# First block of an embedding tower: eight table look-ups by one-hot matmul, half of them in float32 the first time, all tables loaded at once

## What is computed

```
e = stack([tbl_f[ids[:, f]] for f in range(26)], axis=1)
c = concatenate((dense[:, None, :], e), axis=1)          # 2048 x 27 x 128
pairs = einsum('bfd,bgd->bfg', c, c)[:, iu, ju]           # 351 per sample
h = concatenate([dense, pairs, dense], axis=1)
h = maximum(h @ W_top1 + b_top1, 0); h = maximum(h @ W_top2 + b_top2, 0); y = h @ W_top3
```

## Time and profile before

| | us |
|---|---|
| median of 3 runs | 412.22 |
| profiled execution | 411.75 |
| its span | 409.9 |
| PE busy | 380.7 |
| DVE busy | 244.0 |
| POOL busy | 275.5 |
| ACT busy | 221.1 |

### The profile page before, as it was taken

The page is one execution under the profiler, slowest core; times in us unless marked ns, Lnnn a source line. Parts: engine busy times, 40 slices in busy tenths (PEclk is TensorE's granted clock), DMA queues, the critical chain, the costliest instruction groups (busy, mean ns, idle before and its releaser), DMA issues.

```text
span 409.9 us, 8420 instructions
## 1 busy us (share of the span) xinstructions
PE 380.7 (93%) x3248; PEld 371.3 (91%) x3248; DVE 244.0 (60%) x684; ACT 221.1 (54%) x461; POOL 275.5 (67%) x296
## 2 busy tenths in 40 slices
PE   0396699999999999999999999999999999999996
PEld 0395699999999999999999999999999999999885
DVE  4599868375593847467484737657395747621422
ACT  2256276557375546647365546647464555637531
POOL 4777777777777777777777777777777777760000
PEclk9979999999999999999999999999999999999999
DMA  7986833323322333333332333333333332220000
GB/s 164 274 223 136 215 86 87 80 74 91 72 77 69 88 79 80 83 73 83 85 77 69 83 82 74 91 73 80 72 79 81 85 77 62 57 53 1 2 0 2
DMA packets 25732, 35.02 MB, mean 85 GB/s; under 512 B 8710, under 2 KB 19478, under 8 KB 25693
## 3 DMA queue, kind: packets, MB, share of 16 engines
q0 software_dynamic: 9216, 18.89, 19.3%
q1 hardware_dynamic: 14396, 15.45, 15.7%
q10 hardware_dynamic: 2080, 0.15, 0.4%
HBM read 34.45 MB, written 0.01 MB: 84 GB/s over the span
## 4 chain that ended last, share of the span: by engine, by line
PE 86%; DVE 5%; ACT 3%; DMA 2%; issue 1%; SPq 1%
PE look L442 28%; PE prod L469 27%; PE mlp L487 10%; PE turn L453 7%; PE mlp L498 6%; PE mlp L489 3%; DMA dense<-in_dense_rows 2%; DVE onehot L356 2%; PE mlp L506 2%; DVE table_lo L404 1%; ACT feats L280 1%; PE mlp L479 1%; ACT diag L295 1%; PE prod L548 1%; ACT table_hi L268 1%
## 5 line engine op out<-in xcount | busy, mean ns | idle before, releaser
L260 POOL DMA_INDIRECT rows<-in_tbl,ids x288 | 274.7, 954 | 91.3 <-issue 84.8
L356 DVE TENSOR_SCALAR onehot<-wanted,row_no 125x256 fp32r<-125x256 int32 x528 | 164.0, 381 | 18.8 <-PE look L442 18.3
L295 ACT ACTIVATE diag<-prod 32x216 f32<-32x216 f32 x256 | 87.6, 342 | 144.4 <-PE prod L469 142.2
L442 PE MATMUL look<-onehot,table_hi 125*128 125x256 f32 x528 | 137.4, 297 | 23.0 <-DVE table_lo L404 18.3
L442 PE MATMUL look<-onehot,table_lo 125*128 125x256 f32 x528 | 131.9, 287 | 0.0
L469 PE MATMUL prod<-feats 128*128 128x108 f32 x1024 | 124.1, 274 | 1.8 <-ACT feats L280 1.1
L442 PEld LDWEIGHTS look<-onehot,table_hi 125*128 125x128 f32 x528 | 103.1, 195 | 24.6 <-issue 24.6
L469 PEld LDWEIGHTS prod<-feats 128*128 128x128 f32 x1024 | 119.5, 192 | 2.6 <-ACT feats L280 1.4
L442 PEld LDWEIGHTS look<-onehot,table_lo 125*128 125x128 f32 x528 | 103.4, 196 | 0.0
L379 DVE TENSOR_SCALAR h<-mlp,b_sb 128x128 f32<-128x128 f32 x90 | 26.0, 344 | 128.2 <-PE mlp L489 83.4
L280 ACT ACTIVATE feats<-turn 128x512 f32<-128x512 f32 (+1 forms) x80 | 78.4, 1021 | 1.4 <-PE turn L453 0.2
(11 more groups left out here) (39 smaller groups left out, 89.6 us busy)
## 6 DMA issues: line engine op xcount, KB each, us to landing
wanted<-in_small_ids SPq DMA_DIRECT2D x64, 128.0 KB, 3.4
rows<-in_tbl,ids POOLq DMA_INDIRECT x288
feats<-in_tbl SPq DMA_DIRECT2D x7, 448.0 KB
dense<-in_dense_rows SPq DMA_DIRECT2D x16, 64.0 KB, 3.3
w_sb<-in_w_pairs SPq DMA_DIRECT2D x1, 702.0 KB
feats<-in_tbl SPq DMA_DIRECT2D x1, 560.0 KB
w_sb<-in_w SPq DMA_DIRECT2D x1, 512.0 KB
feats<-in_tbl SPq DMA_DIRECT2D x7, 52.0 KB
```

Of the source, the lines that this page charges most:

```text
L260: gp.indirect_dma_start(rows[:, q % SLOTS_OF_ROWS, f * D:(f + 1) * D], None, large_tables[g + f], bass.IndirectOffsetOnAxis(ap=ids[:, t, g ...
L295: last = nc.scalar.activation(diag[t % 2][W * i:W * (i + 1), s * SEG_GROUPS * SLOTS:(s + 1) * SEG_GROUPS * SLOTS], prod_part(prod[s % 2], ...
L356: made = nc.vector.tensor_scalar(onehot[v % 2][:, c - row_nos_at(h), :], wanted[v % WANTED][0:CP, :], row_no[:, c:c + 1], None, ALU.is_equal)
L442: last = nc.tensor.matmul(look[:, 0:BS], part_of(part, k)[:, c * D:(c + 1) * D], onehot[v % 2][:, c, :], start=(c == 0 and part is table_h ...
```

## The change

The tables 1, 3, 5 and 7 are, in the first block, multiplied whole in float32 (one float32 matmul per chunk), and their two parts are made later, for the second block. All eight tables have a place of their own and a semaphore each: seven in `feats` (tiles 2 and 3), the one of 1250 rows in `table`. SP issues tables 4 to 7 right after the dense tile 0 and the id rows 4 to 7 after them, then the dense weights. The lookups of the first block alternate between the banks `look` and `mlp`. The clearing of the pads of tiles 2 and 3 moves behind the last second part; the copy of lookup 8 and the products of tile 2 wait for it. ScalarE's list of the first block is written out in a new order. The core of the diff:

```diff
+WHOLE_FIRST = (1, 3, 5, 7)
-RAW = 4
...
         def raw_table(k):
-            at = (2 + k % RAW // 2) * FT + k % 2 * (FT // 2)
-            return feats[0:CP, at:at + CH[k] * D]
+            if CH[k] == MAX_CH:
+                return table[0:CP, 0:CH[k] * D]
+            return feats[0:CP, 2 * FT + k * CH[k] * D:2 * FT + (k + 1) * CH[k] * D]
...
+        def look_bank(v):
+            return mlp if v < NS and v % 2 else look
...
             def load_table(k):
-                if k >= RAW:
-                    sp.wait_ge(lo_ready, k - RAW + 1)
-                else:
-                    sp.wait_ge(pads_ready, k // 2 + 1)
...
-            for k in range(RAW):
+            for k in range(WANTED):
                 load_wanted(k)
                 load_table(k)
             load_dense(0)
+            for k in range(WANTED, NS):
+                load_table(k)
+            for k in range(WANTED, NS):
+                load_wanted(k)
             sp.dma_start(w1_sb[:, PC * H1:], w_dense).then_inc(w_dense_in, 16)
             sp.dma_start(w_add[:, :], w_dense2).then_inc(w_dense_in, 16)
-            for k in range(RAW, NS):
-                load_wanted(k)
-                load_table(k)
...
             def empty_lookup(v):
                 act.wait_ge(look_full, v + 1)
+                if v == NS:
+                    act.wait_ge(pads_ready, FEAT_TILES)
...
             round_table(0)
+            round_table(2)
+            empty_lookup(0)
+            round_table(1)
+            empty_lookup(1)
+            round_table(4)
+            empty_lookup(2)
+            empty_turn(0, 0)
+            round_table(3)
+            empty_lookup(3)
             place_dense(0)
-            for k in range(NS):
-                if k + 1 < NS:
-                    round_table(k + 1)
-                empty_lookup(k)
-                if 1 <= k <= NC:
-                    empty_turn(0, k - 1)
+            round_table(6)
+            empty_lookup(4)
+            empty_turn(0, 1)
+            round_table(5)
+            empty_lookup(5)
+            empty_turn(0, 2)
+            empty_lookup(6)
+            empty_turn(0, 3)
+            round_table(7)
+            empty_lookup(7)
+            empty_turn(0, 4)
...
             for k in range(NS):
                 one_hot(k)
-                dve.wait_ge(hi_ready, k + 1)
-                nc.vector.tensor_tensor(part_of(table_lo, k), raw_table(k), part_of(table_hi, k).bitcast(F32),
-                                        ALU.subtract).then_inc(lo_ready, 1)
+                if k not in WHOLE_FIRST:
+                    second_part(k)
+            second_part(1)
             one_hot(NS)
+            second_part(3)
+            second_part(5)
+            second_part(7)
+            for k in range(NS):
+                dve.wait_ge(lo_ready[k], 1)
+            dve.wait_ge(look_full, NS)
+            for i in range(2, FEAT_TILES):
+                nc.vector.memset(slots_of(i)[:, SLOTS:W, :], 0.0).then_inc(pads_ready, 1)
             dve.wait_ge(w_dense_in, 32)
...
             def look_up(v):
                 k = v % NS
-                if v < NS:
-                    pe.wait_ge(hi_ready, k + 1)
-                    pe.wait_ge(lo_ready, k + 1)
+                if v == k and k in WHOLE_FIRST:
+                    pe.wait_ge(raw_in[k], 32)
+                elif v == k or v == NS + k and k in WHOLE_FIRST:
+                    pe.wait_ge(hi_ready[k], 1)
+                    pe.wait_ge(lo_ready[k], 1)
                 pe.wait_ge(onehot_ready, v + 1)
-                if v:
+                if v >= NS:
                     pe.wait_ge(look_read, v)
+                elif v >= 2:
+                    pe.wait_ge(look_read, v - 1)
+                if v == k and k in WHOLE_FIRST:
+                    for c in range(CH[k]):
+                        last = nc.tensor.matmul(look_bank(v)[:, 0:BS], raw_table(k)[:, c * D:(c + 1) * D],
+                                                onehot[v % 2][:, c, :].bitcast(F32), start=(c == 0), stop=(c == CH[k] - 1))
+                else:
```

More of the change, by code:

```diff
@@ L124, in tower_program @@
         wanted_in = [sem(f"wanted_in{i}") for i in range(WANTED)]
-        raw_in = [sem(f"raw_in{i}") for i in range(RAW)]
+        raw_in = [sem(f"raw_in{i}") for i in range(NS)]
         dense_in = [sem(f"dense_in{i}") for i in range(DENSE)]
@@ L135, in tower_program @@
         pads_ready = sem("pads_ready")
-        hi_ready = sem("hi_ready")
-        lo_ready = sem("lo_ready")
+        hi_ready = [sem(f"hi_ready{i}") for i in range(NS)]
+        lo_ready = [sem(f"lo_ready{i}") for i in range(NS)]
         onehot_ready = sem("onehot_ready")
@@ L191, in load_table @@
             def load_table(k):
-                if k >= RAW:
-                    sp.wait_ge(lo_ready, k - RAW + 1)
-                else:
-                    sp.wait_ge(pads_ready, k // 2 + 1)
                 src = small_tables[k].rearrange("(p c) d -> p (c d)", c=CH[k])
                 for a, b in ((0, 112), (112, CP)):
-                    sp.dma_start(raw_table(k)[a:b, :], src[a:b, :]).then_inc(raw_in[k % RAW], 16)
+                    sp.dma_start(raw_table(k)[a:b, :], src[a:b, :]).then_inc(raw_in[k], 16)
             def load_dense(t):
@@ L266, in round_table @@
             def round_table(k):
-                act.wait_ge(raw_in[k % RAW], 32 * (k // RAW + 1))
-                nc.scalar.activation(part_of(table_hi, k), raw_table(k), ACT.Copy).then_inc(hi_ready, 1)
+                act.wait_ge(raw_in[k], 32)
+                nc.scalar.activation(part_of(table_hi, k), raw_table(k), ACT.Copy).then_inc(hi_ready[k], 1)
             def empty_lookup(v):
                 act.wait_ge(look_full, v + 1)
+                if v == NS:
+                    act.wait_ge(pads_ready, FEAT_TILES)
                 at = v // NS % 2 * JT * FT
                 nc.scalar.activation(feats[:, at:at + JT * FT].rearrange("d (b w) -> d w b", w=W)[:, 1 + v % NS, :],
-                                     look[:, 0:BS], ACT.Copy)\
+                                     look_bank(v)[:, 0:BS], ACT.Copy)\
                     .then_inc(look_read, 1)
@@ L358, in one_hot, with second_part @@
                 made.then_inc(onehot_ready, 1)
+            def second_part(k):
+                dve.wait_ge(hi_ready[k], 1)
+                nc.vector.tensor_tensor(part_of(table_lo, k), raw_table(k), part_of(table_hi, k).bitcast(F32),
+                                        ALU.subtract).then_inc(lo_ready[k], 1)
             def make_table(t):
@@ L391, in finish_second_layer @@
                 last.then_inc(h2_ready, 1)
-            for i in range(2, FEAT_TILES):
+            for i in range(2):
                 nc.vector.memset(slots_of(i)[:, SLOTS:W, :], 0.0).then_inc(pads_ready, 1)
             nc.vector.memset(one[:, :], 1.0).then_inc(one_made, 1)
-            for i in range(2):
-                nc.vector.memset(slots_of(i)[:, SLOTS:W, :], 0.0).then_inc(pads_ready, 1)
             dve.wait_ge(row_no_made, len(set(CH)))
@@ L433, in look_up @@
                 k = v % NS
-                if v < NS:
-                    pe.wait_ge(hi_ready, k + 1)
-                    pe.wait_ge(lo_ready, k + 1)
+                if v == k and k in WHOLE_FIRST:
[3 more added lines that the diff above has]
+                    pe.wait_ge(lo_ready[k], 1)
                 pe.wait_ge(onehot_ready, v + 1)
-                if v:
+                if v >= NS:
                     pe.wait_ge(look_read, v)
[L440 to L444, removed]
+                elif v >= 2:
[5 more added lines that the diff above has]
+                else:
+                    for c in range(CH[k]):
+                        for part in (table_hi, table_lo):
+                            last = nc.tensor.matmul(look_bank(v)[:, 0:BS], part_of(part, k)[:, c * D:(c + 1) * D],
+                                                    onehot[v % 2][:, c, :], start=(c == 0 and part is table_hi),
+                                                    stop=(c == CH[k] - 1 and part is table_lo))
                 last.then_inc(look_full, 1)
@@ L458, in products @@
                 m = SEGS * t + s
+                if m == 2 * SEGS:
+                    pe.wait_ge(pads_ready, FEAT_TILES)
                 if s == 0:
@@ L510, in _ @@
             pe.wait_ge(ident_ready, 1)
-            pe.wait_ge(pads_ready, FEAT_TILES)
+            pe.wait_ge(pads_ready, 2)
             for k in range(NS):
```

## The result

The changed kernel takes 419.22 us (median of 4 runs, 418.6 to 419.94), the one before 412.0 on the same chip: a ratio of 1.0178 (95%: 1.0154 to 1.0201). It is slower, as forecast, but by 7.2 us instead of 4.0, beyond the range. The profiled execution took 418.89, with a span of 417.1, 7.2 above the 409.9 of before. On some chips the kernel before itself took about 531 us, and what ran there (experiment 9) is compared with it there alone.

What follows compares the result with a forecast made beforehand. PE was taken to bound the bulk, so only S could move: 48.8 from the late id row and chain, plus 2.6 for the clock, gives 51.4, +4.0 us on 411.75: 415.8 us, range 410.2 to 418.2.

Steps and rivals of the forecast that it cites:

- S: Start of the products of tile 0, 47.4 us in the kernel before; forecast to move to 51.4.
- 362.5 us, which the change does not touch: Stretch from S to the end of the span, claimed to stay as it was.
- if the stretch after the first products changes: Stated sign that the prediction is wrong; the stretch from S to the end was expected at 362 to 363 us.
- Cover of about 1 us; without it the cost is a like amount: DVE after indicator 7: 12 us to the end of indicator 9, which PE needs after 13 us; claimed no cost.
- (c), the queue: SP's queue serves in order, so id row 4, behind all eight tables, lands between 26.6 and 28.1, taken as 27.5.
- the 0.8 from the earlier issue: First table issued earlier, no longer held back by clearing pads; takes 0.8 us off the landing of id row 4.
- From indicator 4 to S: First-block chain of indicators, lookups and ACT copies from 27.5 at full clock, giving S = 48.8 before any clock fall.
- Rival 3: Float32 records cost only 0.12 us, lookups 5 and 7 are 3.6 shorter; about 411.4 us, no change; chance 0.09.
- The clock: PE idle from 25 to 31 drops the clock to half, slowing lookups 4 and 5; +2.6 us on S.
- the choice of a third: Share taken of the 3.3 us that lookup 5 could lose at the half clock, since the clock might return.
- Rival 2, rows in time: Id row 4 in by 22, indicator 4 directly after lookup 2; S about 43, 407.4 us; chance 0.17.
- an advance of more than 6 to 7 us would be lost there: Limit on any gain: gathers issued every 1.25 us; judged from the gather of 66.28 feeding the turn at 75.26.

Runs made afterwards that it cites:

- experiment 9: Variants with later weight loads or later turns of tile 0, set against a kernel before that took 530.7 to 532 us; ratios 0.980 to 1.003, inconclusive.
- Experiment 6: The changed kernel with the sum of the dense weights on DVE behind indicator 9 instead of ahead of it; one execution, 418.87 us.
- experiment 2: The changed kernel with each late id row ahead of its table and ACT's copies in the order of the turns; 414.26 us, ratio 1.0042.
- 3: The changed kernel with only ACT's copies put in the order of the turns, id rows still late; 414.92 us, ratio 1.0082.
- experiment 1: The changed kernel with SP issuing each id row 4 to 7 ahead of its table; 413.02 us, ratio 1.0019.
- 4: The changed kernel with all tables split, no float32 lookups, ACT's list in plain order, id rows still late; 414.12 us, ratio 1.0047.
- 5: The changed kernel with all tables split, no float32 lookups, ACT's list in plain order, id rows between the tables; 410.77 us, ratio 0.994.
- experiment 7: The changed kernel with SP holding tables 4 to 7 and the id rows behind them until four lookups are done; one execution, 426.45 us.
- 8: The kernel before with ACT placing dense tile 0 after lookup 3 instead of ahead of the rounding of table 1; 410.59 us, ratio 0.995.

## Why the prediction was right in its sign and wrong in its size

The forecast was 3.2 us short (+4.0 against +7.2). S accounts for 0.7 of that: 51.4 forecast, 52.14 measured, with two larger errors in it that nearly cancel, which was luck. The other 2.5 come from the step that put everything behind S at nothing, "362.5 us, which the change does not touch": it measured 364.96, and without that the time would have lain in the range. The prediction's own sign of being wrong, "if the stretch after the first products changes", came true. Term by term:

- **"362.5 us, which the change does not touch" failed:** it is 2.46 longer, 0.81 in tile 0 and 1.65 in the tail.
  - Tile 0: "Cover of about 1 us; without it the cost is a like amount". The cover was not there. From the end of indicator 7 to that of indicator 9 it took 13.1 us instead of 12, with gaps of 0.87 and 0.60 ahead of DVE's clears that the sum had left out, and PE wanted it after 12.8: lookup 9 waited 0.54. Experiment 6 took the +0.81 away. In 2 and 3, where PE no longer waits for ACT's copies between lookup 7 and S, lookup 9 waited longer, 1.33 and 1.22: part of what S gains is paid back there.
  - The tail: true of the work, not of the clock. It was at the half clock (+1.65), in a stretch that no edit touches; so it was in experiment 2 (4.57 for the same 24 products), and not in 1 and 3 to 8. On the chip of experiments 1 to 4 the kernel before alone ranged over 22 runs from 410.5 to 414.8 us, with mean granted clocks of 1.0 down to 0.983. Why it fell in this place stays open.
- **(c), the queue: right mechanism, mis-sized.** Indicator 4 started at 29.70, not at 27.5: +2.2, the largest single error. That queue order made the wait is shown by experiment 1. Most of the error lies in the starting point. The sum took 3.03 MB to be in at 19.9 - 0.8 = 19.1; in the kernel after, 3.02 MB were in at 20.9, when the rounding of table 4 stopped waiting. The dense tile has the same bytes ahead of it in both kernels; 17.7 - 0.8 = 16.9 was implied, and it landed at 7.01 + 11.5 = 18.5. The rest, 1.80 MB in 8.8 us, 0.205 MB/us, was within the 7.5 to 9 us of the sum. So the 0.8 from the earlier issue was never gained. A transfer that the sum left out, the gathers' indices on ACT's queue, took 10.4 us beside these tables where it took 6.3 before; whether that is what held them up was not tried. Issues of the kernel after from 0 to 12 us, KB and us to landing:

```profile
ids<-in_gather_ids ACTq DMA_DIRECT2D x1, 135.0 KB, 10.4
dense<-in_dense_rows SPq DMA_DIRECT2D x1, 64.0 KB, 11.5
```

- **From indicator 4 to S:** 23.9 forecast (51.4 - 27.5), 22.44 measured. The waits for ACT were there (1.67, 1.68, 1.16), float32 lookup 5 took 3.47 us for 16 records (0.217 each, forecast 3.5), lookup 7 4.48 for 20. Rival 3 is ruled out. Of the 1.5 us that it came out shorter, 1.1 are the clock's.
- **The clock:** it fell at about 29.5, PE having stopped at 27.82; but only lookup 4 was slow (3.46), lookup 5 ran at the full clock. +1.5, not +2.6, which hides half of (c)'s error. In experiment 6, with the same first block, it stayed at half until past 42 and S was 2.4 later: the choice of a third was a guess, and either outcome was to be had.
- **Rival 2, rows in time:** its condition was made true in experiment 1, and S was 45.93, not 43. Its limit was named ("an advance of more than 6 to 7 us would be lost there") but taken from a tile without backlog: the 0.9 and "over 1 its flight" are together 6.6 to 7.5 in the first block, and 2.2 to 2.3 only with SP's queue empty, so the limit was nearer.

## What to carry to other kernels

A small transfer behind a long row of large ones in one queue arrives when the row is through: add up the bytes ahead of it, divide by a rate measured between two arrivals, and check the starting point as well as the rate, with everything that flies beside it. Gathers on another queue are late too while that row lasts (here 7 us instead of 2.3). Before work is moved off the critical path, find the next thing that is due there (here copies on ACT, then gathers); and look for a wait at the head of an engine's list, as the dense tile was, before a redesign. Work moved off one chain lands on another: count its cover to the microsecond, or expect to pay for it. And give a stretch that "nothing touches" a width: here the clock alone moved it by 1.65 us.

## What the runs showed of the hardware beyond what was expected

- A gather of 64 KB needs 6.6 to 7.5 us from the start of its issue to its last packet while SP's queue is full, and 2.2 to 2.3 us when it is empty (experiment 7). Turns that waited for one started 7.4 to 8.6 us after its issue did, over the kernel after and experiments 1 to 6 and 8.
- Gathers whose issue starts inside a second part on DVE last longer. POOL's timeline of the kernel after, against second parts at 9.38 (1.23 long), 17.23 (1.21) and 49.62 (2.40):

```profile
9.89 1.53 POOL L263 DMA_INDIRECT rows<-in_tbl,ids  x1 [0.30 <-issue]
...
17.97 1.29 POOL L263 DMA_INDIRECT rows<-in_tbl,ids  x1 [0.31 <-issue]
...
50.88 1.96 POOL L263 DMA_INDIRECT rows<-in_tbl,ids  x1 [0.30 <-issue]
```

  They end at 11.42, 19.26 and 52.84, each 0.81 to 0.82 after the second part does; nearly all others take 0.94 (the one of 53.14, inside the second part that ends at 53.42, took 1.10). In the kernel before, gathers that started within 0.02 us of a second part's start also took 0.94.
- A float32 record of 256 columns takes 0.217 us at the full clock, a split one 0.12: a chunk in float32 (two records) costs 1.8 times a split one.
